# Layer 0 of a two-layer attention kernel: a branch hint on VectorE's loop, and the matmuls of a row in another order

## The chip, the cores and the metric

One core of a Trainium2 chip runs the whole program. The metric is device microseconds from launch to end. The kernel before ran three times: median 5077.78 us (5075.72 to 5081.89). One further execution was profiled: 5074.54 us, with a span of 5072.7 us from its first to its last instruction.

## The reference

The input is an image `x` of 128 channels by 256 by 256. Layer 0 is the stage that changes:

```
n      = layer_norm_over_all(group_norm(x)) * ln_w + ln_b      # 128 x 256 x 256
q, k, v = wq @ n, wk @ n, wv @ n      # over channels: 4 heads of 64, at each image row i and position
g      = sigmoid(wg @ n + wg_b)
bias   = wb @ n                       # 4 x 256 x 256
a      = softmax over m of (q[i, j] . k[i, m] / 8 + bias[h, j, m])
o      = g * (a @ v)
x      = x + wrep @ o + wrep_b
```

The bias of the scores is one table of 4 heads x 256 x 256, the same for all rows. Layer 1 is a second attention (8 heads of 32 channels) over the same image with a group norm before it; it is not touched.

## The kernel before, in words

The program has five stages, one after the other: weights are prepared; a first pass over the image gathers statistics and projects the bias parts; the statistics are finished; `layer0` (L456) works through the 256 image rows; then the statistics of its output are finished and `layer1` (L882) follows.

`layer0` handles one image row (256 positions, 128 channels) at a time. Each engine has a program of its own, a list of calls for "row k" in which a call may belong to row k, k+1, k+2 or k+3. So the engines work on up to four rows at once, and the order of the calls in each engine's `row` function, written out by hand, is the order of its queue. Engines are tied by counting semaphores alone. `over_rows` (L53) unrolls eight rows, peels the first and the last eight, and runs the 30 groups between in a loop; each engine has its own loop and its own branch at the end.

For one row the work is this.

- GpSimd (POOL) makes the normalised row in six steps: `normalise` part 0 subtracts the mean, part 1 multiplies with the inverse deviation, 2 and 3 apply `ln_w` and `ln_b`, 4 and 5 split the result into a high and a low float32r half. It also divides the exponentials by their sums (`divide`, L537, one call for each of the four heads).
- TensorE (PE) makes queries, keys, values and gates (`queries`, `keys`, `values`, `gates`, six matmuls of 256 columns each, since a product of split numbers is three products), then `scores` for a pair of heads (12 matmuls, two heads side by side on 64 rows of the array each), `transposes` of the probabilities of one head (4), `attend` for a pair of heads (two heads side by side on 64 columns each) and `project_out` (6).
- ScalarE (ACT) rounds queries and keys to their high halves (`queries_high`, `keys_high`), copies values, takes the gates' tanh (`gates_out`), the exponentials (`exponents`, two units a head), the high half of the gated result (`output_high`) and two of the four transposed heads (`transposed_out`, heads 0 and 2).
- VectorE (DVE) adds the bias to the scores and takes their maximum (`biased`, two units a head), makes the low halves (`queries_low`, `keys_low`, `output_low`), the reciprocals (`inverse`), the other two transposed heads (`transposed_out`, 1 and 3), the gated product (`gated`), the residual sum (`residual`) and the statistics of the result (`measure`).
- SyncE issues the loads of `x`, `ln_w` and `ln_b` (two rows a transfer, buffers for eight rows) and the stores of the result.

The eight PSUM banks are shared out by hand: bank 0 holds queries and then values (`b_qv`), bank 1 keys and then gates (`b_kg`), banks 2 and 3 the scores of one head each of a pair (`b_s`), banks 4 and 5 the transposes (`b_t`), bank 6 the attend products (`b_av`), bank 7 the output (`b_out`). The second pair's scores wait until the first pair's banks are evacuated, and `probs_t`, the evacuated transposes, has one buffer a head.

PE's order for a row is: attend pair 1 of k; transposes 1 of k+1; scores pair 0, gates of k+2; queries of k+3; attend pair 0 of k+1; scores pair 1 of k+2; transposes 3 and 2 of k+1; keys of k+3; output of k; values of k+3; transposes 0 of k+2.

Of the kernel before, what the change touches and what calls it, by code (L numbers as in the profile page):

```python
# [20 lines left out]
P = 128  # L21
C0 = 128
W = 256
# [21 lines left out]
def loop_ends_peeled(engine, count, body):  # L45

    body(0, True, False)
    with engine.Fori(1, count - 1) as t:
        body(t, False, False)
    body(count - 1, False, True)  # L50

def over_rows(engine, total, unroll, row, ahead=3, behind=1):  # L53

    def body(t, first, last):
        for k in range(-ahead if first else 0, unroll + behind if last else unroll):
            row(t, k, lambda d, k=k: (not first or k + d >= 0) and (not last or k + d < unroll))
    loop_ends_peeled(engine, total // unroll, body)  # L60
# [395 lines left out]
def layer0(nc, m, x, ln_w, ln_b, x1, stats):  # L456

    UNROLL, TILE = 8, 2  # L460
    BUFS = UNROLL // TILE
    AHEAD = 4
    PAIRS = NH0 // 2
    with ExitStack() as ctx:
# [12 lines left out]
        probs_t = sb("probs_t", [P, NH0, KC, W])  # L477
# [8 lines left out]
        b_qv, b_kg = m.psum[0], m.psum[1]  # L486
        b_s, b_t, b_av, b_out = m.psum[2:4], m.psum[4:6], m.psum[6], m.psum[7]
# [9 lines left out]
        av_mm = sems("av_mm", PAIRS)  # L497
# [4 lines left out]
        def rows(engine, row):  # L502
            over_rows(engine, W, UNROLL, row, ahead=AHEAD, behind=1)

# [31 lines left out]
        def _(pool):  # L536
# [59 lines left out]
        def _(pe):  # L596
            def queries(t, k):
# [3 lines left out]
                wait(pe, v_ready, r)  # L601
                for j in range(HC):
                    last = matmul_split(nc, b_qv[:, j * W:(j + 1) * W], [w[:, 0, j] for w in m.wqk], [x_[:, k % 4] for x_ in xn])
# [11 lines left out]
            def values(t, k):  # L615
                r = UNROLL * t + k
                pe.wait_ge(q_ready, r + 1)
                for c in range(KC):
                    last = matmul_split(nc, b_qv[:, c * W:(c + 1) * W], [x_[:, k % 4, c * P:(c + 1) * P] for x_ in xn], [w[:] for w in m.wv_t])
# [9 lines left out]
            def scores(t, k, pair):  # L629
# [9 lines left out]
                for c in range(KC):  # L639
                    for a, b in ((0, 0), (0, 1), (1, 0)):  # L640
                        for j in range(2):
                            channels = slice(j * D0, (j + 1) * D0)
                            last = nc.tensor.matmul(b_s[j][:, c * W:(c + 1) * W], q[a][channels, k % 2, pair, c * P:(c + 1) * P],  # L643
                                                    kk_[b][channels, k % 2, pair], start=a + b == 0, stop=a == 1)
                last.then_inc(s_mm[pair], 1)

            def transposes(t, k, h):
                r = UNROLL * t + k
                pe.wait_ge(p_ready[h], r + 1)
                if h >= 2:  # L650
                    pe.wait_ge(t_ready[h - 2], r + 1)
                else:
                    wait(pe, t_ready[h + 2], r)
                for kc in range(KC):
                    for qc in range(KC):
                        last = nc.tensor.transpose(b_t[h % 2][:, kc * W + qc * P:kc * W + (qc + 1) * P], probs[:, h, qc, kc * P:(kc + 1) * P], m.ident[:])  # L656
                last.then_inc(t_mm[h], 1)

            def attend(t, k, pair):
                r = UNROLL * t + k  # L660
                for j in range(2):
# [3 lines left out]
                for kc in range(KC):  # L665
                    for j in range(2):
                        h = 2 * pair + j
                        last = nc.tensor.matmul(b_av[D0 * j:D0 * (j + 1), pair * W:(pair + 1) * W], v[:, k % 2, kc, h * D0:(h + 1) * D0],  # L668
                                                probs_t[:, h, kc], start=kc == 0, stop=kc == KC - 1)
                last.then_inc(av_mm[pair], 1)  # L670

            def project_out(t, k):
                r = UNROLL * t + k
                pe.wait_ge(o_split, r + 1)
                wait(pe, y_ready, r)
                for c in range(HC):
                    last = matmul_split(nc, b_out[:, 0:W], [w[:, c, :] for w in m.wrep_t], [part[:, c] for part in o_parts], start=c == 0, stop=c == HC - 1)
                last.then_inc(out_mm, 1)

            def row(t, k, has):  # L680
                if has(0):
# [716 lines left out]
```

## Time and profile before

| what | value |
|---|---|
| median of three runs | 5077.78 us |
| profiled execution, time | 5074.54 us |
| profiled execution, span | 5072.7 us |
| PE busy, share of the span | 4726.3 us, 93% |
| DVE busy | 4027.1 us, 79% |
| ACT busy | 3552.5 us, 70% |
| POOL busy | 3459.8 us, 68% |
| mean granted TensorE clock | 0.971 |
| landing of layer 0's loads (`x`, `ln_w`, `ln_b`), median | 2.9, 3.4, 3.6 us |

Busy shares are means over stages with different limits. Layer 0 takes roughly the half of the span that ends near 3003 us. In a timeline a line is one instruction, or some merged ones (x8): its start, its duration, engine, source line, operation and tiles; in brackets how long the engine stood idle before it and what ended that. Durations of neighbours overlap, since an engine takes the next instruction before the last one's result is written: what an instruction costs its queue is the distance from its start to the next start.

### The profile page before, as it was taken

What the parts mean: (1) busy time and instruction counts of PE and PEld (TensorE: products, weight loads), DVE (VectorE), ACT (ScalarE), POOL (GpSimd) and SP (SyncE); (2) the same over time, 40 slices, a digit from 0 to 9 for tenths busy, and PEclk for the clock granted to TensorE, in tenths of its full rate; (3) what the DMA queues carried; (4) which work ended last, traced back from release to release, by engine and by line L of the source; (5) the groups of instructions that cost most, each with busy time, mean ns of one, the idle gap of its engine ahead of it and who ended that gap; (6) DMA issues with size and microseconds to landing.
All of it is one profiled execution on the core that took longest, in us unless ns stands there. A gap on an engine that the chain in (4) does not pass through costs nothing. (4 is left out here: it accounts for less than half of the span.)

```text
span 5072.7 us, 150113 instructions
## 1 busy us (share of the span) xinstructions
PE 4726.3 (93%) x44087; PEld 3890.6 (77%) x44087; DVE 4027.1 (79%) x12779; ACT 3552.5 (70%) x11216; POOL 3459.8 (68%) x5926
## 2 busy tenths in 40 slices
PE   4664999999999999999999979999999999999999
PEld 2332878778787787787877857888888888888887
DVE  4445888888888888888888887888888888888887
ACT  2332888888888888888888856666666666666665
POOL 2333888888788888788878845666666666666665
PEclk8776999999999999999999989999999999999999
DMA  8993111111111111111111101111111111111111
GB/s 329 360 359 135 56 54 51 57 50 58 50 58 51 50 58 50 58 50 55 54 50 58 50 26 48 54 50 50 50 50 50 50 53 53 50 50 50 50 50 44
DMA packets 237474, 383.70 MB, mean 76 GB/s; under 512 B 18756, under 2 KB 156616, under 8 KB 224968
## 3 DMA queue, kind: packets, MB, share of 16 engines
q1 hardware_dynamic: 237256, 381.63, 22.5%
q14 instruction: 183, 1.50, 0.1%
q8 instruction: 35, 0.57, 0.0%
HBM read 309.21 MB, written 72.35 MB: 75 GB/s over the span
## 5 line engine op out<-in xcount | busy, mean ns | idle before, releaser
L1300 POOL TENSOR_SCALAR l_probs<-l_probs,l_inv 128x256 f32<-128x256 f32 x2048 | 943.3, 478 | 737.5 <-DVE l_inv L1205 731.9
L543 POOL TENSOR_SCALAR l_probs<-l_probs,l_inv 128x256 f32<-128x256 f32 x2048 | 982.1, 492 | 475.1 <-DVE l_inv L795 475.1
L1124 ACT ACTIVATE l_probs<-bank,l_neg_max 128x256 f32<-128x256 f32 x2048 | 947.4, 481 | 487.2 <-DVE l_neg_max L1199 487.2
L714 ACT ACTIVATE l_probs<-l_probs,l_neg_max 128x256 f32<-128x256 f32 x2048 | 1012.3, 503 | 6.3 <-DVE l_neg_max L787 6.3
L787 DVE CUSTOM_DVE_ANT_0 l_probs<-bank,bias 128x256 f32<-128x256 f32 x2048 | 749.6, 421 | 263.1 <-PE bank L656 187.0
L1199 DVE TENSOR_REDUCE l_neg_max<-bank 128x2 f32<-128x512 f32 x1024 | 646.1, 683 | 93.4 <-PE bank L1033 93.4
L1212 DVE TENSOR_TENSOR l_probs_t<-bank,bias 128x512 f32<-128x512 f32 x1024 | 674.0, 681 | 36.0 <-PE bank L1043 10.4
L656 PE MATMUL bank<-ident,l_probs 128*128 128x128 f32 x4096 | 603.9, 280 | 1.4 <-POOL l_probs L543 1.1
L668 PE MATMUL bank<-l_probs_t,l_v 128*64 128x256 f32 x4096 | 555.1, 392 | 38.9 <-DVE l_probs_t L809 38.3
L656 PEld LDWEIGHTS bank<-ident,l_probs 128*128 128x128 f32 x4096 | 444.7, 141 | 135.5 <-issue 99.0
L1043 PE MATMUL bank<-ident,l_probs 128*128 128x128 f32 x4096 | 531.8, 273 | 3.4 <-DVE l_probs_t L1212 1.7
L1043 PEld LDWEIGHTS bank<-ident,l_probs 128*128 128x128 f32 x4096 | 460.0, 141 | 6.0 <-POOL l_probs L1300 3.6
L1124 ACT ACTIVATION_READ_ACCUMULATOR l_probs<-bank,l_neg_max 128x1 f32 x2048 | 436.1, 213 | 0.0
L714 ACT ACTIVATION_READ_ACCUMULATOR l_probs<-l_probs,l_neg_max 128x1 f32 x2048 | 399.6, 195 | 0.0
L668 PEld LDWEIGHTS bank<-l_probs_t,l_v 128*64 128x64 f32 x4096 | 251.2, 136 | 189.8 <-issue 85.8
L747 ACT ACTIVATE l_gate<-bank,wg_b_half 128x256 f32<-128x256 f32 x512 | 214.1, 469 | 233.7 <-PE bank L81 233.7
L754 ACT ACTIVATE l_probs_t<-bank 128x512 f32<-128x512 f32 x512 | 301.0, 588 | 95.0 <-PE bank L656 95.0
L643 PE MATMUL bank<-l_k_high,l_q_high 64*128 64x256 f32 x2048 | 343.3, 330 | 13.0 <-DVE l_neg_max L787 13.0
L809 DVE COPY l_probs_t<-bank 128x512 f32<-128x512 f32 x512 | 343.3, 670 | 1.1 <-PE bank L656 1.1
L79 PE MATMUL bank<-l_xn_high,wqk_high 128*128 128x256 f32 x1024 | 309.5, 302 | 25.4 <-POOL l_xn_low L570 25.4
L340 POOL TENSOR_TENSOR fp_x<-fp_x,fp_ln_w 128x2048 f32<-128x2048 f32 x32 | 145.5, 4548 | 263.4 <-DVE chunk_stats L327 263.4
L79 PE MATMUL bank<-l_xn_high,w_qk_high 128*128 128x256 f32 x1024 | 310.5, 303 | 3.5 <-POOL l_xn_low L1289 3.5
(193 smaller groups left out, 14046.6 us busy)
## 6 DMA issues: line engine op xcount, KB each, us to landing
fp_x<-in_x_dram SPq DMA_DIRECT2D x32, 1024.0 KB, 6.9
fp_ln_w<-in_L_conv_ln_w_dram SPq DMA_DIRECT2D x32, 1024.0 KB, 8.9
fp_ln_b<-in_L_conv_ln_b_dram SPq DMA_DIRECT2D x32, 1024.0 KB, 10.5
fp_pair<-in_L_conv_pair_repr_dram SPq DMA_DIRECT2D x32, 1024.0 KB, 12.8
l_x<-in_x_dram SPq DMA_DIRECT2D x128, 256.0 KB, 2.9
l_ln_w<-in_L_conv_ln_w_dram SPq DMA_DIRECT2D x128, 256.0 KB, 3.4
l_ln_b<-in_L_conv_ln_b_dram SPq DMA_DIRECT2D x128, 256.0 KB, 3.6
x<-l_y SPq DMA_DIRECT2D x128, 256.0 KB, 2.0
```

Of the source, the lines that this page charges most:

```text
L79: nc.tensor.matmul(out, lh, rh, start=start, stop=False)
L543: last = nc.gpsimd.tensor_scalar(probs[:, h, c], probs[:, h, c], inv[:, h, c:c + 1], 1.0, ALU.mult, ALU.mult)
L643: last = nc.tensor.matmul(b_s[j][:, c * W:(c + 1) * W], q[a][channels, k % 2, pair, c * P:(c + 1) * P], kk_[b][channels, k % 2, pair], sta ...
L656: last = nc.tensor.transpose(b_t[h % 2][:, kc * W + qc * P:kc * W + (qc + 1) * P], probs[:, h, qc, kc * P:(kc + 1) * P], m.ident[:])
L668: last = nc.tensor.matmul(b_av[D0 * j:D0 * (j + 1), pair * W:(pair + 1) * W], v[:, k % 2, kc, h * D0:(h + 1) * D0], probs_t[:, h, kc], sta ...
L714: last = nc.scalar.activation(probs[:, h, c], probs[:, h, c], ACT.Exp, bias=neg_max[:, h, c:c + 1], scale=-1.0, accum_out=total[:, h, c:c ...
L787: last = nc.vector.tensor_tensor_reduce(out=probs[:, h, c], in0=b_s[h % 2][:, c * W:(c + 1) * W], in1=m.bias0[:, c, h], scale=-1.0, scalar ...
L1043: last = nc.tensor.transpose(b_t[TURNS.index(h) % 2][:, kc * W + qc * P:kc * W + (qc + 1) * P], probs[:, h, qc, kc * P:(kc + 1) * P], m.id ...
L1124: last = nc.scalar.activation(probs[:, h, c], b_s[h % 4][:, c * W:(c + 1) * W], ACT.Exp, bias=neg_max[:, h, c:c + 1], accum_out=total[:, h ...
L1199: nc.vector.tensor_reduce(neg_max[:, h], b_s[h % 4][:].rearrange("p (a c) -> p a c", a=KC), AX.X, ALU.max, negate=True).then_inc(max_ready, 1)
L1212: nc.vector.tensor_tensor(probs_t[:, k % 2, h], b_t[TURNS.index(h) % 2][:].rearrange("p (a c) -> p a c", a=KC), m.bias1[:, :, h], ALU.add) ...
L1300: last = nc.gpsimd.tensor_scalar(probs[:, h, c], probs[:, h, c], inv[:, h, c:c + 1], 1.0, ALU.mult, ALU.mult)
```

## The change

- Scores: one call makes all four heads' scores into four banks (2 to 5), with one semaphore `s_mm` in place of one for each pair. It waits for the evacuation of all four heads of the row before.
- Attend: one call makes all four heads' products, with one semaphore `av_mm`.
- Transposes: one bank (6) in place of two. The transposes of a head wait until the head before (in the order 2, 3, 0, 1) is copied out. `probs_t` has two buffers, by the parity of the row.
- Output: the output projection goes into bank 0, which queries and values use as well (`b_qvo`). Queries wait for the residual sum of two rows back, and the output projection for the values' evacuation two rows ahead.
- All five hand-written orders change. POOL runs five rows ahead (`AHEAD = 5`), keys four rows. The number and the sizes of matmuls, activations and vector operations of a row are the same.

```diff
-def loop_ends_peeled(engine, count, body):
+def loop_ends_peeled(engine, count, body, hinted=None):
+
 
     body(0, True, False)
-    with engine.Fori(1, count - 1) as t:
+    with hinted.Fori(1, count - 1, engines=[engine.engine], hint_back_edge=True) if hinted else engine.Fori(1, count - 1) as t:
         body(t, False, False)
     body(count - 1, False, True)
 
 
-def over_rows(engine, total, unroll, row, ahead=3, behind=1):
+def over_rows(engine, total, unroll, row, ahead=3, behind=1, hinted=None):
 
 
 
     def body(t, first, last):
         for k in range(-ahead if first else 0, unroll + behind if last else unroll):
             row(t, k, lambda d, k=k: (not first or k + d >= 0) and (not last or k + d < unroll))
-    loop_ends_peeled(engine, total // unroll, body)
+    loop_ends_peeled(engine, total // unroll, body, hinted)
...
     UNROLL, TILE = 8, 2
     BUFS = UNROLL // TILE
-    AHEAD = 4
+    AHEAD = 5
+    OUT_BEHIND = 2
     PAIRS = NH0 // 2
...
-        probs_t = sb("probs_t", [P, NH0, KC, W])
+        probs_t = sb("probs_t", [P, 2, NH0, KC, W])
...
-        b_qv, b_kg = m.psum[0], m.psum[1]
-        b_s, b_t, b_av, b_out = m.psum[2:4], m.psum[4:6], m.psum[6], m.psum[7]
+        b_qvo, b_kg = m.psum[0], m.psum[1]
+        b_s, b_t, b_av = m.psum[2:6], m.psum[6], m.psum[7]
...
-        s_mm = sems("s_mm", PAIRS)
+        s_mm, av_mm = sem("s_mm"), sem("av_mm")
...
             def row(t, k, has):
-                if has(2):
-                    normalise(t, k + 2, 4)
-                if has(3):
-                    normalise(t, k + 3, 0)
-                if has(2):
-                    normalise(t, k + 2, 5)
-                if has(0):
-                    divide(t, k, 3)
-                if has(3):
-                    normalise(t, k + 3, 1)
-                if has(0):
-                    divide(t, k, 2)
-                if has(3):
-                    normalise(t, k + 3, 2)
-                if has(1):
-                    divide(t, k + 1, 0)
-                if has(3):
-                    normalise(t, k + 3, 3)
-                if has(1):
-                    divide(t, k + 1, 1)
+                if has(5):
+                    normalise(t, k + 5, 0)
+                if has(4):
+                    normalise(t, k + 4, 4)
+                if has(5):
+                    normalise(t, k + 5, 1)
+                if has(4):
+                    normalise(t, k + 4, 5)
+                if has(2):
+                    divide(t, k + 2, 0)
+                    divide(t, k + 2, 1)
+                if has(5):
+                    normalise(t, k + 5, 2)
+                if has(2):
+                    divide(t, k + 2, 2)
+                    divide(t, k + 2, 3)
+                if has(5):
+                    normalise(t, k + 5, 3)
             rows(pool, row)
...
-                wait(pe, v_ready, r)
+                if isinstance(r, int) and r <= OUT_BEHIND:
+                    wait(pe, v_ready, r)
+                else:
+                    pe.wait_ge(y_ready, r - OUT_BEHIND)
...
             def scores(t, k):
-                for h in range(2):
-                    if pair:
-                        pe.wait_ge(s_ready[h], r + 1)
-                    else:
-                        wait(pe, s_ready[2 + h], r)
+                for h in range(NH0):
+                    wait(pe, s_ready[h], r)
...
             def transposes(t, k, h):
-                if h >= 2:
-                    pe.wait_ge(t_ready[h - 2], r + 1)
-                else:
-                    wait(pe, t_ready[h + 2], r)
+                wait(pe, t_ready[(h - 1) % NH0], r + 1 if h else r)
...
-            def attend(t, k, pair):
-                r = UNROLL * t + k
-                for j in range(2):
-                    pe.wait_ge(t_ready[2 * pair + j], r + 1)
+            def attend(t, k):
+                r = UNROLL * t + k
+                for h in range(NH0):
+                    pe.wait_ge(t_ready[h], r + 1)
...
             def project_out(t, k):
-                wait(pe, y_ready, r)
+                if not isinstance(r, int) or r + OUT_BEHIND < W:
+                    pe.wait_ge(v_ready, r + OUT_BEHIND + 1)
+                else:
+                    pe.wait_ge(y_ready, r)
...
             def row(t, k, has):
-                if has(0):
-                    attend(t, k, 1)
-                if has(1):
-                    transposes(t, k + 1, 1)
-                if has(2):
-                    scores(t, k + 2, 0)
-                    gates(t, k + 2)
-                if has(3):
-                    queries(t, k + 3)
-                if has(1):
-                    attend(t, k + 1, 0)
-                if has(2):
-                    scores(t, k + 2, 1)
-                if has(1):
-                    transposes(t, k + 1, 3)
+                if has(1):
                     transposes(t, k + 1, 2)
-                if has(3):
-                    keys(t, k + 3)
                 if has(0):
                     project_out(t, k)
+                if has(1):
+                    transposes(t, k + 1, 3)
+                if has(3):
+                    gates(t, k + 3)
+                    queries(t, k + 3)
+                if has(1):
+                    attend(t, k + 1)
+                if has(2):
+                    transposes(t, k + 2, 0)
+                if has(3):
+                    scores(t, k + 3)
+                if has(2):
+                    transposes(t, k + 2, 1)
                 if has(3):
                     values(t, k + 3)
-                if has(2):
-                    transposes(t, k + 2, 0)
+                if has(4):
+                    keys(t, k + 4)
             rows(pe, row)
...
             def transposed_out(t, k, h):
                 r = UNROLL * t + k
                 act.wait_ge(t_mm[h], r + 1)
-                wait(act, av_mm[h // 2], r)
-                nc.scalar.activation(probs_t[:, h], b_t[h % 2][:].rearrange("p (a c) -> p a c", a=KC), ACT.Copy).then_inc(t_ready[h], 1)
+                wait(act, av_mm, r - 1)
+                nc.scalar.activation(probs_t[:, k % 2, h], b_t[:].rearrange("p (a c) -> p a c", a=KC), ACT.Copy).then_inc(t_ready[h], 1)
 
             def row(t, k, has):
-                if has(0):
-                    output_high(t, k)
-                if has(2):
-                    gates_out(t, k + 2)
-                if has(3):
-                    queries_high(t, k + 3)
+                if has(3):
+                    keys_high(t, k + 3)
+                if has(1):
+                    transposed_out(t, k + 1, 2)
                 if has(2):
                     exponents(t, k + 2, 0)
                     exponents(t, k + 2, 1)
-                if has(1):
-                    transposed_out(t, k + 1, 2)
-                if has(3):
-                    keys_high(t, k + 3)
+                if has(3):
+                    queries_high(t, k + 3)
                 if has(2):
                     exponents(t, k + 2, 2)
                     exponents(t, k + 2, 3)
                     transposed_out(t, k + 2, 0)
                 if has(3):
+                    gates_out(t, k + 3)
+                if has(1):
+                    output_high(t, k + 1)
+                if has(3):
                     values_out(t, k + 3)
             rows(act, row)
...
-                    last = nc.vector.tensor_tensor_reduce(out=probs[:, h, c], in0=b_s[h % 2][:, c * W:(c + 1) * W], in1=m.bias0[:, c, h], scale=-1.0,
+                    last = nc.vector.tensor_tensor_reduce(out=probs[:, h, c], in0=b_s[h][:, c * W:(c + 1) * W], in1=m.bias0[:, c, h], scale=-1.0,
...
             def row(t, k, has):
-                if has(1):
-                    inverse(t, k + 1, 2)
-                if has(0):
-                    gated(t, k)
-                if has(1):
-                    inverse(t, k + 1, 3)
-                    transposed_out(t, k + 1, 1)
                 if has(2):
                     biased(t, k + 2, 1)
-                    biased(t, k + 2, 0)
-                if has(0):
-                    output_low(t, k)
-                if has(3):
-                    queries_low(t, k + 3)
-                if has(2):
-                    inverse(t, k + 2, 0)
-                    biased(t, k + 2, 3)
-                    biased(t, k + 2, 2)
-                    inverse(t, k + 2, 1)
-                if has(1):
-                    transposed_out(t, k + 1, 3)
+                if has(3):
+                    keys_low(t, k + 3)
                 if has(0):
                     residual(t, k)
-                if has(3):
-                    keys_low(t, k + 3)
+                if has(1):
+                    transposed_out(t, k + 1, 3)
+                if has(2):
+                    inverse(t, k + 2, 0)
+                    biased(t, k + 2, 2)
+                    biased(t, k + 2, 3)
+                if has(3):
+                    queries_low(t, k + 3)
+                if has(2):
+                    inverse(t, k + 2, 1)
                 if has(0):
                     measure(t, k)
-            rows(dve, row)
+                if has(1):
+                    gated(t, k + 1)
+                if has(2):
+                    inverse(t, k + 2, 3)
+                    inverse(t, k + 2, 2)
+                if has(3):
+                    biased(t, k + 3, 0)
+                if has(2):
+                    transposed_out(t, k + 2, 1)
+                if has(1):
+                    output_low(t, k + 1)
+            rows(dve, row, hinted=nc)
```

## Rows read from the trace of the kernel before

**Rows 1.** The page, its first line.

```profile
span 5072.7 us, 150113 instructions
```

**Rows 2.** Busy time of each engine (with its records) in a stretch of layer 0.

```profile
1000.00:2500.00 1500.00, 1466.97 (x13080) 1192.40 (x13080) 1244.17 (x4716) 1222.82 (x3651) 1218.97 (x2130) 1.00 0.17 54
```

**Rows 3.** Timeline of PE: the first matmuls of each block of a steady row.

```profile
1005.41 1.08 PE L668 MATMUL bank<-l_probs_t,l_v 128*64 128x256 f32 x8
1006.43 0.66 PE L656 MATMUL bank<-ident,l_probs 128*128 128x128 f32 x4
1007.01 0.39 PE L643 MATMUL bank<-l_k_high,l_q_high 64*128 64x256 f32 x2
...
1007.71 0.28 PE L643 MATMUL bank<-l_k_high,l_q_low 64*128 64x256 f32 x2
1007.91 0.39 PE L79 MATMUL bank<-l_xn_high,wg_t_high 128*128 128x256 f32 x1
...
1008.73 0.28 PE L79 MATMUL bank<-l_xn_high,wqk_high 128*128 128x256 f32 x1
...
1009.53 1.08 PE L668 MATMUL bank<-l_probs_t,l_v 128*64 128x256 f32 x8
1010.54 0.39 PE L643 MATMUL bank<-l_k_high,l_q_high 64*128 64x256 f32 x2
...
1011.45 1.09 PE L656 MATMUL bank<-ident,l_probs 128*128 128x128 f32 x8
1012.30 0.36 PE L79 MATMUL bank<-l_xn_high,wqk_high 128*128 128x256 f32 x1
...
1013.09 0.28 PE L79 MATMUL bank<-l_o_high,wrep_t_high 128*128 128x256 f32 x1
...
1014.49 0.60 PE L656 MATMUL bank<-ident,l_probs 128*128 128x128 f32 x4
1015.02 1.08 PE L668 MATMUL bank<-l_probs_t,l_v 128*64 128x256 f32 x8
```

**Rows 4.** Timeline of DVE: first instructions of an iteration, and of a later one.

```profile
1047.71 0.17 DVE L795 RECIPROCAL l_inv<-l_total 128x2 f32<-128x2 f32 x1 [2.92 <-issue]
...
1048.53 0.67 DVE L809 COPY l_probs_t<-bank 128x512 f32<-128x512 f32 x1
...
1283.89 0.17 DVE L795 RECIPROCAL l_inv<-l_total 128x2 f32<-128x2 f32 x1 [2.94 <-issue]
```

**Rows 5.** Timeline of PE behind the end of an iteration.

```profile
1049.30 1.08 PE L668 MATMUL bank<-l_probs_t,l_v 128*64 128x256 f32 x8 [1.27 <-DVE l_probs_t L809]
```

**Rows 6.** Waits of DVE, 580 to 3000 us: total, times, longest.

```profile
DVE l_inv L795 <- issue: 85.0, 29, 3.2
```

**Rows 7.** Timeline of DVE in two steady rows.

```profile
1008.17 0.42 DVE L787 CUSTOM_DVE_ANT_0 l_probs<-bank,bias 128x256 f32<-128x256 f32 x1 [0.27 <-PE bank L643]
...
1013.70 0.67 DVE L809 COPY l_probs_t<-bank 128x512 f32<-128x512 f32 x1
1014.29 0.48 DVE L833 SCALAR_TENSOR_TENSOR l_y<-bank,wrep_b,l_x 128x256 f32<-128x256 f32 x1
1014.68 0.68 DVE L803 TENSOR_TENSOR l_k_low<-bank,l_k_high 128x512 fp32r<-128x512 f32 x1
```

**Rows 8.** Timeline of ACT: its copy of a transposed head.

```profile
1012.58 0.60 ACT L754 ACTIVATE l_probs_t<-bank 128x512 f32<-128x512 f32 x1 [0.37 <-PE bank L656]
```

**Rows 9.** `output_low` (L822): min/median/max ns of all 256; one beside POOL's timeline.

```profile
L822 DVE TENSOR_TENSOR l_o_low<-l_o,l_o_high x256: 685/1009/1018, 500.7 to 3002.7; 128x512 fp32r<-128x512 f32 x128
...
1107.47 0.69 DVE L822 TENSOR_TENSOR l_o_low<-l_o,l_o_high 128x512 fp32r<-128x512 f32 x1
...
1107.47 1.03 POOL L543 TENSOR_SCALAR l_probs<-l_probs,l_inv 128x256 f32<-128x256 f32 x1
1108.47 0.74 POOL L561 TENSOR_TENSOR l_xf<-l_xf,l_ln_w 128x256 f32<-128x256 f32 x1
1109.52 0.93 POOL L543 TENSOR_SCALAR l_probs<-l_probs,l_inv 128x256 f32<-128x256 f32 x2 [0.31 <-DVE l_inv L795]
```

More of the change, by code:

```diff
@@ L500, in layer0, with rows @@
         block = ctx.enter_context(nc.Block())
-        def rows(engine, row):
-            over_rows(engine, W, UNROLL, row, ahead=AHEAD, behind=1)
+        def rows(engine, row, hinted=None):
+            over_rows(engine, W, UNROLL, row, ahead=AHEAD, behind=1, hinted=hinted)
         @block.sync
@@ L600, in queries @@
                 pe.wait_ge(xn_ready, r + 1)
-                wait(pe, v_ready, r)
+                if isinstance(r, int) and r <= OUT_BEHIND:
+                    wait(pe, v_ready, r)
+                else:
+                    pe.wait_ge(y_ready, r - OUT_BEHIND)
                 for j in range(HC):
-                    last = matmul_split(nc, b_qv[:, j * W:(j + 1) * W], [w[:, 0, j] for w in m.wqk], [x_[:, k % 4] for x_ in xn])
+                    last = matmul_split(nc, b_qvo[:, j * W:(j + 1) * W], [w[:, 0, j] for w in m.wqk], [x_[:, k % 4] for x_ in xn])
                 last.then_inc(q_mm, 1)
@@ L618, in values @@
                 for c in range(KC):
-                    last = matmul_split(nc, b_qv[:, c * W:(c + 1) * W], [x_[:, k % 4, c * P:(c + 1) * P] for x_ in xn], [w[:] for w in m.wv_t])
+                    last = matmul_split(nc, b_qvo[:, c * W:(c + 1) * W], [x_[:, k % 4, c * P:(c + 1) * P] for x_ in xn], [w[:] for w in m.wv_t])
                 last.then_inc(v_mm, 1)
@@ L627, in gates, with scores @@
                 last.then_inc(g_mm, 1)
-            def scores(t, k, pair):
+            def scores(t, k):
                 r = UNROLL * t + k
@@ L633, in scores @@
                 pe.wait_ge(k_ready, r + 1)
-                for h in range(2):
-                    if pair:
-                        pe.wait_ge(s_ready[h], r + 1)
-                    else:
-                        wait(pe, s_ready[2 + h], r)
-                for c in range(KC):
-                    for a, b in ((0, 0), (0, 1), (1, 0)):
-                        for j in range(2):
[L642 to L645, printed above, removed]
+                for h in range(NH0):
+                    wait(pe, s_ready[h], r)
+                for pair in range(PAIRS):
+                    for c in range(KC):
+                        for a, b in ((0, 0), (0, 1), (1, 0)):
+                            for j in range(2):
+                                channels = slice(j * D0, (j + 1) * D0)
+                                last = nc.tensor.matmul(b_s[2 * pair + j][:, c * W:(c + 1) * W], q[a][channels, k % 2, pair, c * P:(c + 1) * P],
+                                                        kk_[b][channels, k % 2, pair], start=a + b == 0, stop=a == 1)
+                last.then_inc(s_mm, 1)
             def transposes(t, k, h):
@@ L649, in transposes @@
                 pe.wait_ge(p_ready[h], r + 1)
-                if h >= 2:
-                    pe.wait_ge(t_ready[h - 2], r + 1)
-                else:
-                    wait(pe, t_ready[h + 2], r)
+                wait(pe, t_ready[(h - 1) % NH0], r + 1 if h else r)
                 for kc in range(KC):
                     for qc in range(KC):
-                        last = nc.tensor.transpose(b_t[h % 2][:, kc * W + qc * P:kc * W + (qc + 1) * P], probs[:, h, qc, kc * P:(kc + 1) * P], m.ident[:])
+                        last = nc.tensor.transpose(b_t[:, kc * W + qc * P:kc * W + (qc + 1) * P], probs[:, h, qc, kc * P:(kc + 1) * P], m.ident[:])
                 last.then_inc(t_mm[h], 1)
-            def attend(t, k, pair):
+            def attend(t, k):
                 r = UNROLL * t + k
-                for j in range(2):
-                    pe.wait_ge(t_ready[2 * pair + j], r + 1)
+                for h in range(NH0):
+                    pe.wait_ge(t_ready[h], r + 1)
                 pe.wait_ge(v_ready, r + 1)
                 wait(pe, o_ready, r)
[L665 to L670, printed above, removed]
+                for pair in range(PAIRS):
+                    for kc in range(KC):
+                        for j in range(2):
+                            h = 2 * pair + j
+                            last = nc.tensor.matmul(b_av[D0 * j:D0 * (j + 1), pair * W:(pair + 1) * W], v[:, k % 2, kc, h * D0:(h + 1) * D0],
+                                                    probs_t[:, k % 2, h, kc], start=kc == 0, stop=kc == KC - 1)
+                last.then_inc(av_mm, 1)
             def project_out(t, k):
@@ L720, in queries_high @@
                 act.wait_ge(q_mm, r + 1)
-                wait(act, s_mm[1], r - 1)
-                nc.scalar.activation(q[0][:, k % 2], b_qv[:].rearrange("p (h c) -> p h c", h=HC), ACT.Copy).then_inc(q_high, 1)
+                wait(act, s_mm, r - 1)
+                nc.scalar.activation(q[0][:, k % 2], b_qvo[:].rearrange("p (h c) -> p h c", h=HC), ACT.Copy).then_inc(q_high, 1)
             def keys_high(t, k):
@@ L726, in keys_high @@
                 act.wait_ge(k_mm, r + 1)
-                wait(act, s_mm[1], r - 1)
+                wait(act, s_mm, r - 1)
                 nc.scalar.activation(kk_[0][:, k % 2], b_kg[:].rearrange("p (h c) -> p h c", h=HC), ACT.Copy).then_inc(k_high, 1)
@@ L738, in values_out @@
                 act.wait_ge(v_mm, r + 1)
-                wait(act, av_mm[1], r - 1)
-                nc.scalar.activation(v[:, k % 2], b_qv[:].rearrange("p (h c) -> p h c", h=2), ACT.Copy).then_inc(v_ready, 1)
+                wait(act, av_mm, r - 1)
+                nc.scalar.activation(v[:, k % 2], b_qvo[:].rearrange("p (h c) -> p h c", h=2), ACT.Copy).then_inc(v_ready, 1)
             def gates_out(t, k):
```

22 lines of the change are left out of this document (11 added, 11 removed).

## The prediction

> **What bounds the kernel now.** I read the busy time by stretch first, then the timelines of one loop iteration on PE, DVE and ACT, then DVE's waits. In the middle of layer 0, which ends near 3003 us [rows 9], TensorE (PE) is busy 97.8% of the time (1466.97 of 1500 us) at the full granted clock, while VectorE (DVE), ScalarE (ACT) and GpSimd (POOL) each stand at 81 to 83% [rows 2]. So a row costs what PE needs for it, and the others matter where PE waits for them.
>
> A steady row on PE is 9.61 us: from the attend of a second pair at 1005.41 to the next at 1015.02, with no idle between [rows 3]. Eight rows are 76.88 us. An iteration of the loop takes more: DVE's first instruction of one starts at 1047.71 and that of the third after it at 1283.89, which is 78.73 us each [rows 4]. The missing 1.85 us is at the end of the loop body. There DVE stands still for 2.92 us with no releaser ("issue") ahead of the first reciprocal of the next iteration. Its copy of turned probabilities is then late, and PE waits 1.27 us for it [rows 4, 5]. DVE pays this 29 times, 85.0 us in all [rows 6]: the back edges of a loop of 30 iterations. PE has its own copy of the loop and shows no stop at its end.
>
> **The change on PE.** The matmuls stay the same; their order changes, and what one costs depends on its neighbour. From [rows 3], start to start: attend of a pair 1.02 and 1.01; transposes of one head 0.58 after an attend and 0.53 before one, and 0.85 for two heads together, so 0.43 a head among full tiles; scores of a pair 0.90 and 0.91; gates 0.82 after scores; queries 0.80 before attend; keys 0.79 after transposes; output and values 1.40, so 0.70 each behind another projection. Sum: 1.02 + 0.58 + 0.90 + 0.82 + 0.80 + 1.01 + 0.91 + 0.85 + 0.79 + 1.40 + 0.53 = 9.61.
>
> New order, by those rows: transposes of head 2, 0.43; output after transposes 0.79; transposes 3, 0.43; gates 0.79; queries before attend 0.80; all attend products 1.87; transposes 0, 0.58; all scores 1.61; transposes 1, 0.43; values 0.79; keys 0.70. For the attend products I take one pair's 1.01 and add its four inner steps of about 0.215, the longer first and last steps being paid once; for the scores 0.91 and six unbroken steps of 0.117 (0.70 us lie between the first and the last of six, 1007.01 and 1007.71, the first step being the longer one by 0.1). Sum 9.22. The 0.39 us come from fewer changes between tiles of 64 rows, 64 columns and full size, less two more starts behind transposes. Four score banks also free the second pair from the evacuation of the first, but in a steady row nothing waits for that now.
>
> The Trainium skill, "TensorEngine Tiling (Array Packing)", says that changing the tiling mode drains TensorE. The trace agrees: these are the places where a step is some 0.1 us longer.
>
> **What then is late.** At 9.22 us a row I place the other queues against PE's, each instruction at its predecessor's start plus its interval. Three chains come near.
>
> First, the one bank for transposes. ACT must have copied head 2's out before head 3's are made, and only the output projection lies between: 1.22 us from start to start. The copy starts 1.13 us after a block of eight transposes (1011.45 to 1012.58 [rows 3, 8]), so 0.70 after one of four; it takes 0.60, and its release 0.1 at most: 1.38. PE loses 0.16, and a row is at least 9.38 us. The other three handoffs have over 1.4 us of other work between.
>
> Second, DVE. Its queue is now: biased 1, keys_low, residual, copy 3, inverse 0, biased 2 and 3, queries_low, inverse 1, measure, gated, two inverses, biased 0 of the next row, copy 1, output_low, and round to biased 1. Gates on PE wait for keys_low, which stands behind four instructions that start only when the scores of the row before are there. Once round: gates' start to scores' start 0.79 + 0.80 + 1.87 + 0.58 = 4.04; scores' start to biased 0, 1.61 - 0.21 + 0.46 = 1.86 (last score matmul to DVE, 1007.71 to 1008.17 [rows 3, 7]); biased 0, 0.69 (four units from 1008.17, two heads, in 1.38: output_low starts at once behind); copy 0.59 (1013.70 to 1014.29); output_low x; biased 1, 0.69; keys_low 0.68 [rows 7]; DVE's end to PE's start 0.10 (copy at 1048.53 plus 0.67, attend at 1049.30 [rows 4, 5]). Together 8.65 + x. Queries_low ends about 3.0 us after gates' start, 1.0 before scores want it, and copy 3 some 0.5 before attend does, so neither decides. ACT and POOL are busy 8.0 us of a row of 9.84 on average [rows 2] and keep over 1 us of gap.
>
> What is x? output_low reads two operands from SBUF. It takes 0.69 at least (0.60 to the next start) and mostly 1.009 (0.92) [rows 9]. In one fast case it starts together with a division on POOL, which then takes 1.03 alone, where two take 0.93 a little later: one of the two stands still. So x lies between 0.60 and 0.92. In the new order output_low falls beside normalise 3 and 0, back to back on POOL, so I take 0.85, nearer the row that is seen most. A row is then 9.50.
>
> The Trainium skill, "SBUF — State Buffer", section "SBUF: two separate sides", calls the port pair that DVE and GpSimd share an exclusive lock, held for the whole instruction. The trace's pair agrees; by that rule output_low could wait for a whole GpSimd instruction, which is the slow rival below.
>
> Third, the output projection of a row waits for its output_low, with only transposes 2 ahead; by the same placement it is released 0.25 us late, inside the 0.28 that PE would lose to keys_low anyway. Output and queries share a bank now; residual ends 0.5 us before queries want it, and nothing is lost there.
>
> **The hint**, if it works, takes DVE's gap away: 29 x 1.85 = 53.7 us off. Something may stay, since the branch now lies in the chain that binds (between output_low and biased 1). No row shows it: below, nothing; above, 0.45, a small part of today's gap; I take 0.2, 5.8 us in all. **The ends:** POOL works five rows ahead instead of four and keys four instead of three, so one more short row fills the pipeline: between 0 and one row, 9; I take 3. **Loads** for a row go out seven rows ahead as now and are first read five rows ahead instead of three. Two rows, 19 us, remain for a landing of a few us, so they cost nothing; without that cover a late landing would stop POOL, then keys.
>
> **Sum.** Rows: 256 x 0.11 = 28.2 off. Hint: 53.7 - 5.8 = 47.9 off. Ends +3. Net -73.1 against the profiled execution's 5074.5 (span 5072.7 [rows 1] and 1.8 around it), 5001.4. The median of the runs lies 3.3 above that execution, so 5005.
>
> **Rivals.**
> *DVE's chain does not bind.* With output_low alone, x = 0.60 gives 9.25, and the transposes' handoff sets 9.38: 256 x 0.23 = 58.9, plus 53.7, less 3: 4968. Against it: 1.009 is the median of 256. Were that handoff hidden too, 9.22 would give 4927.
>
> *The gap stays at the back edge.* DVE has 30 records a row there, ACT 23, POOL 14 [rows 2], and only DVE's gap shows; the hint may bring the branch's target and leave the part behind it missing. Then 2.94 lies in the binding chain: 29 x (2.94 - 1.85) = 31.6 more, less 28.2, plus 3: 5084. For it: no slack on DVE in the new order. Against it: the gap is at the branch and nowhere else now.
> The Trainium skill, "Runtime: NRT & Kernel Launch", section "Instruction fetch mechanics", says that a taken branch to a target outside the two blocks held pays a fetch, and names no remedy.
>
> *Slower: DVE waits for whole POOL instructions.* If output_low meets the start of a POOL instruction of 0.74 us each row [rows 9], x = 1.34 and a row is 9.99: 256 x 0.38 = 97.3, less 47.9, plus 3: 5130. It decides from a row of 9.82, x = 1.17, where the hint is used up. Against it: no output_low took over 1.018.
>
> *A row of 9.6 to 9.75:* one or two handoffs 0.1 longer than placed, 26 us each: 5030 to 5069.
>
> **Chances.** Forecast 0.50 (its own range 4980 to 5030), chain not binding 0.15 and all hidden 0.04, row of 9.6 to 9.75 0.12, gap stays 0.12, whole POOL instructions 0.07. The range 4960 to 5068 leaves out 0.04 below and at most 0.16 above. A measurement of this kernel can tell some 0.2%, 10 us: faster, below 5068, 0.81; same 0.09 (most of the gap's case); slower 0.10.
>
> **What the profile after would show.** Right: no DVE gap with "issue" once in eight rows; a wait of PE of about 0.3 us a row ahead of gates or output, released by DVE; output_low near 1.0 us; layer 0 some 70 us shorter and layer 1 the same. Wrong: PE idle ahead of transposes 3 on ACT alone (the first chain binds); a wait of scores on queries_low; a DVE gap near 2.9 us every 76; or a gap of ACT's or POOL's own at the back edge, which DVE's would hide today.

## The result, and the profile after

The changed kernel takes 5214.96 us (median of four runs, 5198.22 to 5219.51) against 5079.55 for the kernel before: a ratio of 1.0261, with a 95% interval of 1.0236 to 1.0286. It is 2.6% slower, where 1.5% faster was forecast, and the time lies far outside the range. The profiled execution took 5219.51 us, with a span of 5217.4. One execution of a run below, the one without the hint, took 5542.28 us at a mean granted TensorE clock of 0.82 in place of 0.95, and is left out of its median.

The busy time (with records) of PE, its weight loads, DVE, ACT and POOL in the same stretch of layer 0 as in [rows 2]; the column before the last two is the granted clock:

```profile
1000.00:2500.00 1500.00, 1394.41 (x12402) 1168.31 (x12400) 1260.29 (x4470) 1152.63 (x3458) 1135.34 (x2020) 0.97 0.16 50
```

PE does 12402 matmul records there in place of 13080, and stands at 93% in place of 97.8%. Who keeps it waiting is told by the first line of PE's waits, 500 to 3200 us (total, times, longest):

```profile
PE bank L80 <- DVE l_o_low L821: 182.3, 113, 2.4
```

Before, no such wait stood in layer 0's steady rows. `output_low` is L821 now. Its line, which answers to the first of [rows 9] (min/median/max ns):

```profile
L821 DVE TENSOR_TENSOR l_o_low<-l_o,l_o_high x256: 682/748/3187, 506.0 to 3144.9; 128x512 fp32r<-128x512 f32 x128
```

The median has fallen from 1.009 to 0.748 us and the maximum has risen from 1.018 to 3.187. So the median says nothing here; the longest ones do. Below, an output_low that takes longer because of POOL is called locked out. Two rows of the same execution, from the timelines of DVE and, below the dots, of POOL:

```profile
1065.66 0.73 DVE L821 TENSOR_TENSOR l_o_low<-l_o,l_o_high 128x512 fp32r<-128x512 f32 x1
...
1065.10 0.74 POOL L565 TENSOR_TENSOR l_xf<-l_xf,l_ln_b 128x256 f32<-128x256 f32 x1
1065.80 1.19 POOL L557 TENSOR_TENSOR l_xf<-l_x,mean 128x256 f32<-128x256 f32 x1
```

```profile
1020.83 3.19 DVE L821 TENSOR_TENSOR l_o_low<-l_o,l_o_high 128x512 fp32r<-128x512 f32 x1
...
1020.29 0.75 POOL L565 TENSOR_TENSOR l_xf<-l_xf,l_ln_b 128x256 f32<-128x256 f32 x1
1020.99 0.74 POOL L557 TENSOR_TENSOR l_xf<-l_x,mean 128x256 f32<-128x256 f32 x1
1021.68 0.41 POOL L570 TENSOR_SCALAR l_xn_high<-l_xf 128x256 fp32r<-128x256 f32 x1
1022.05 0.73 POOL L561 TENSOR_TENSOR l_xf<-l_xf,rstd 128x256 f32<-128x256 f32 x1
1022.74 0.73 POOL L572 TENSOR_TENSOR l_xn_low<-l_xf,l_xn_high 128x256 fp32r<-128x256 f32 x1
```

In both, output_low starts 0.54 to 0.56 us behind the start of POOL's normalise 3 (L565). In the first it goes ahead of POOL's next instruction, normalise 0, which then takes 1.19 us in place of 0.74. In the second POOL's next four instructions (normalise 0, 4, 1 and 5) all go first, each at its usual length, and output_low takes its own 0.69 us only when this unbroken run ends. PE, which has nothing ahead of the output projection but head 2's transposes, waits for it:

```profile
1024.07 0.38 PE L80 MATMUL bank<-l_o_high,wrep_t_high 128*128 128x256 f32 x1 [2.31 <-DVE l_o_low L821]
```

From the starts of the 250 successive output_lows between 560 and 3145 us, by their length:

| output_low takes | rows | to the next output_low |
|---|---|---|
| 0.7 to 0.8 us | 140 | 9.36 to 9.46 us, mostly 9.37 (less in the layer's last rows) |
| 1.1 to 1.3 | 16 | 9.73 to 9.88 |
| 1.4 | 26 | 10.03 |
| 3.2 | 68 | 12.68 on average |

The 26 of 1.4 us were passed by one POOL instruction, and the 16 came at the start of normalise 0 and waited for it alone. The rows of the 68 are longer than by their 2.5 us of delay because PE's granted clock fell in some of them: in 25 it stayed at 1.00 and the row took 11.8 us, in 43 it was 0.87 over the row, which took 13.0 to 13.3. Busy time and granted clock behind one wait of each kind:

```profile
1024.00:1027.50 3.50, 3.43 (x28) 3.02 (x30) 3.50 (x16) 1.52 (x5) 0.93 (x2) 1.00 0.22 75
1037.00:1040.50 3.50, 3.50 (x19) 2.98 (x19) 2.51 (x12) 1.00 (x5) 0.93 (x2) 0.51 0.00 0
```

The second stretch is at the lower level, 1.2 GHz, after PE had stood still for 2.31 us; the first is at 2.4 GHz after a wait just as long.

Against rows of 9.37 us the sum is 68 x 3.31 + 26 x 0.66 + 16 x 0.42 = 249 us. Taken from 5215 that leaves 4966; the first rival stood at 4968. The experiments had to show whether this sum is real.

### The profile page after: what moved, and what is told of

Same layout as the page of the kernel before. It is cut to its first block and busy times, and to the rows that moved or that the text cites. A ratio compares the mean times of both kernels' runs of the same rounds, so it can differ in the third digit from the quotient of the medians.

```text
span 5217.4 us, 149629 instructions
## 1 busy us (share of the span) xinstructions
PE 4734.8 (91%) x44087; PEld 3959.4 (76%) x44087; DVE 4169.1 (80%) x12779; ACT 3544.6 (68%) x11216; POOL 3422.6 (66%) x5926
## 5 line engine op out<-in xcount | busy, mean ns | idle before, releaser
L1301 POOL TENSOR_SCALAR l_probs<-l_probs,l_inv 128x256 f32<-128x256 f32 x2048 | 943.7, 478 | 737.4 <-DVE l_inv L1206 731.9
L545 POOL TENSOR_SCALAR l_probs<-l_probs,l_inv 128x256 f32<-128x256 f32 x2048 | 947.8, 478 | 652.5 <-DVE l_inv L794 652.3
L654 PE MATMUL bank<-ident,l_probs 128*128 128x128 f32 x4096 | 659.8, 285 | 5.1 <-ACT l_probs_t L753 1.6
L1044 PE MATMUL bank<-ident,l_probs 128*128 128x128 f32 x4096 | 532.4, 273 | 2.9 <-DVE l_probs_t L1213 1.5
L667 PE MATMUL bank<-l_probs_t,l_v 128*64 128x256 f32 x4096 | 503.5, 388 | 2.2 <-DVE l_probs_t L808 2.2
L667 PEld LDWEIGHTS bank<-l_probs_t,l_v 128*64 128x64 f32 x4096 | 274.0, 138 | 151.7 <-issue 10.4
L821 DVE TENSOR_TENSOR l_o_low<-l_o,l_o_high 128x512 fp32r<-128x512 f32 x256 | 383.3, 1497 | 0.7 <-ACT l_o_high L733 0.7
L80 PE MATMUL bank<-l_o_high,wrep_t_high 128*128 128x256 f32 x512 | 174.9, 342 | 182.3 <-DVE l_o_low L821 182.3
L739 ACT ACTIVATE l_v<-bank 128x512 f32<-128x512 f32 x256 | 153.7, 600 | 270.3 <-PE bank L82 270.3
L644 PE MATMUL bank<-l_k_high,l_q_high 64*128 64x256 f32 x2048 | 315.5, 305 | 2.3 <-DVE l_q_low L798 2.3
L80 PE MATMUL bank<-l_xn_high,wqk_high 128*128 128x256 f32 x1024 | 292.7, 286 | 26.2 <-POOL l_xn_low L572 26.2
## 6 DMA issues: line engine op xcount, KB each, us to landing
fp_pair<-in_L_conv_pair_repr_dram SPq DMA_DIRECT2D x32, 1024.0 KB, 11.8
```

Of the source, the lines that this page charges most:

```text
L80: nc.tensor.matmul(out, lh, rh, start=start, stop=False)
L545: last = nc.gpsimd.tensor_scalar(probs[:, h, c], probs[:, h, c], inv[:, h, c:c + 1], 1.0, ALU.mult, ALU.mult)
L654: last = nc.tensor.transpose(b_t[:, kc * W + qc * P:kc * W + (qc + 1) * P], probs[:, h, qc, kc * P:(kc + 1) * P], m.ident[:])
L821: nc.vector.tensor_tensor(o_parts[1][:], o[:], o_parts[0][:].bitcast(F32), ALU.subtract).then_inc(o_split, 1)
L1044: last = nc.tensor.transpose(b_t[TURNS.index(h) % 2][:, kc * W + qc * P:kc * W + (qc + 1) * P], probs[:, h, qc, kc * P:(kc + 1) * P], m.id ...
L1301: last = nc.gpsimd.tensor_scalar(probs[:, h, c], probs[:, h, c], inv[:, h, c:c + 1], 1.0, ALU.mult, ALU.mult)
```

## The experiments

All ratios are to the kernel before, run on the same chip in the same rounds.

**The hint taken out of the changed kernel.**

```diff
-            rows(dve, row, hinted=nc)
+            rows(dve, row)
```

> The changed kernel with the branch hint taken out. Theory A (output_low is locked out by POOL's unbroken run in about 68 of 256 rows, and that is the whole loss): the 2.9 us gap comes back at 29 back edges in DVE's binding queue, so about 29 x 2.9 = 84 us on top of 5215, near 5300; but POOL runs dry in such a gap, so some lockouts of the rows behind it may go and it may be as low as 5240. Theory B (the hint itself disturbs the loop): as fast as or faster than the changed kernel, 5215 or below.

5366.50 us (median of three, 5366.17 to 5378.63), ratio 1.0575 (1.0554 to 1.0596). The hint is no culprit: without it the kernel loses another 152 us. That is more than 84, and the forecast that some lockouts would go was wrong. There are more of them: of 250 output_lows here 90 take 3.0 to 3.2 us and 96 take 1.4, and against rows of 9.37 the sum is 397 us, 148 more than in the changed kernel. DVE's gap at the back edge is in this sum, but only 21.5 us of it, in 19 places. Why the gap brings more lockouts was not tested; that it shifts DVE against POOL is a guess.

**The hint alone, on the kernel before.** The two helper functions change as in the diff of the change, and then

```diff
-            rows(dve, row)
+            rows(dve, row, hinted=nc)
```

> The kernel before with nothing but the branch hint on the vector engine's loop of layer 0. Both theories of the loss in the row order leave this alone: 29 x 1.85 = 54 us off, 5024, and no gap with issue in DVE's waits. If the hint is what costs (theory B): no faster than before, 5078 or more.

5021.21 us, ratio 0.9886 (0.987 to 0.9903): 60 us off (5080.85 less 5021.21) where 54 were forecast. PE is never idle in the stretch, and every row takes 9.6 us. The hint by itself is worth 1.1%, and DVE's wait with "issue" is gone:

```profile
1000.00:2500.00 1500.00, 1500.00 (x13429) 1218.98 (x13429) 1262.91 (x4843) 1255.66 (x3747) 1264.75 (x2187) 1.00 0.17 55
```

**POOL yields.** POOL's first step for the row five ahead (normalise 0) waits until output_low is done.

```diff
                     wait(pool, xn_ready, r - 1)
+                    if isinstance(r, int):
+                        wait(pool, o_split, r - 4)
+                    else:
+                        pool.wait_ge(o_split, r - 4)
```

> The changed kernel; POOL's first step for a row five ahead also waits until output_low of the present row is done, so that POOL's run has a break just where output_low stands. Same work. Theory A: no output_low over 1.2 us, rows at 9.4 us, the whole at 4965 to 4990, faster than both kernels. Theory C (the long output_low only shows a queue that is bound by the single transpose bank or by gates behind keys_low): PE's waits move to another instruction and the time stays above 5150.

4975.26 us, ratio 0.9793 (0.9777 to 0.981). The wait added to POOL makes the kernel 240 us faster than the changed one, and 106 faster than the one before (5080.85 in these rounds). No output_low takes over 0.93 us. POOL waits 168.2 us in all for it and has the room: it still stands still for reciprocals (284.0 us):

```profile
L825 DVE TENSOR_TENSOR l_o_low<-l_o,l_o_high x256: 680/728/930, 510.3 to 2904.2; 128x512 fp32r<-128x512 f32 x128
```

```profile
POOL l_probs L545 <- DVE l_inv L798: 284.0, 256, 4.0
POOL l_xf L561 <- DVE l_o_low L825: 168.2, 245, 0.7
```

**One operand from PSUM.** The orders stay as they are; output_low's first operand lies in PSUM. It is the product without the gate, so this kernel leaves the gate out of the low half and serves only to measure time. Attend waits for output_low in place of `gated`, since the bank is now read until then.

```diff
-                wait(pe, o_ready, r)      # attend
+                wait(pe, o_split, r)
...
-                nc.vector.tensor_tensor(o_parts[1][:], o[:], o_parts[0]...
+                nc.vector.tensor_tensor(o_parts[1][:], b_av[:]..., o_parts[0]...
```

> The changed kernel, with output_low reading the ungated product from its PSUM bank in place of the gated one from SBUF, so that it has one SBUF input; it leaves the gate out of the low half. Size and queue are the same. Theory A in the form that only an instruction with two SBUF inputs is locked out: output_low is 0.7 us in every row, rows at 9.4 us, 4965 to 4985. If POOL holds back any DVE instruction at that place, or the queue is the cause (theory C): the long ones stay and the time stays near 5215.

4971.78 us, ratio 0.9786 (0.977 to 0.9803). All 256 take 0.68 to 0.69 us. In 252 of them output_low starts during normalise 3, at the median 0.55 us into it as in the changed kernel, and the same unbroken run of POOL follows:

```profile
L821 DVE TENSOR_TENSOR l_o_low<-bank,l_o_high x256: 680/681/692, 509.1 to 2898.1; 128x512 fp32r<-128x512 f32 x128
```

So what holds output_low back is its second SBUF operand, and with one alone the kernel is 243 us faster. Theory C is out by both runs. The Trainium skill, "SBUF — State Buffer", section "SBUF: two separate sides", names just this class, a DVE instruction "with two SBUF inputs" against a GpSimd instruction that reads SBUF, as one that takes the shared pair; the run agrees.

**A shorter run of POOL.** Normalise 3 and 0 stay together; the three steps after them go behind the division of head 0.

```diff
                 if has(5):
                     normalise(t, k + 5, 0)
+                if has(2):
+                    divide(t, k + 2, 0)
                 if has(4):
                     normalise(t, k + 4, 4)
...
                 if has(2):
-                    divide(t, k + 2, 0)
                     divide(t, k + 2, 1)
```

> The changed kernel, with POOL's order altered so that only two instructions (normalise 3 and normalise 0) stand between the place where output_low arrives and POOL's next wait (the division of head 0); the other three follow behind that division. Same work. If a locked-out output_low gets its turn only when POOL runs dry, the longest one shrinks from 3.2 to about 1.4 to 2.3 us, and the time falls from 5215 to between 5000 and 5060. If the 3.2 us are a fixed penalty, or do not depend on POOL's queue, they stay and so does the time.

5267.72 us, ratio 1.037 (1.0352 to 1.0387). The length came out as forecast and the time did not. The longest output_low shrank with the run, from 3.2 us to 2.0 in nearly every row and 2.3 at most; a fixed penalty is out. But now output_low is locked out in 245 of 250 rows instead of 110, and a row takes 10.57 us. One row, DVE then POOL:

```profile
1003.92 1.98 DVE L822 TENSOR_TENSOR l_o_low<-l_o,l_o_high 128x512 fp32r<-128x512 f32 x1
...
1003.92 0.75 POOL L565 TENSOR_TENSOR l_xf<-l_xf,l_ln_b 128x256 f32<-128x256 f32 x1
1004.62 0.73 POOL L557 TENSOR_TENSOR l_xf<-l_x,mean 128x256 f32<-128x256 f32 x1
1008.42 0.93 POOL L545 TENSOR_SCALAR l_probs<-l_probs,l_inv 128x256 f32<-128x256 f32 x2 [3.07 <-DVE l_inv L795]
```

1003.92 + 1.98 - 0.69 = 1005.21, which is 0.14 us before the recorded end of the last instruction of the run (1005.35); in the long row above it is 1020.83 + 3.19 - 0.69 = 1023.33 against 1023.47. A long-delayed output_low gets its turn when POOL's run ends, whether that has two instructions or four behind it. And a lockout that comes every row costs more than a longer one in every fourth: 256 x 1.2 us against 68 x 3.3. I had priced the length and left out that in the new order output_low also arrives elsewhere, at the very start of normalise 3.

**The hint in the new order, with nothing locked out.** The kernel in which POOL yields, and

```diff
-            rows(dve, row, hinted=nc)
+            rows(dve, row)
```

> The kernel in which POOL yields to output_low (4975 us), without the branch hint. It measures what the hint is worth in the new order when nothing is locked out. By the prediction's term (the whole gap of 2.94 us lies in a queue without slack) 29 x 2.9 = 85 us, 5060. The few rows of 11.0 us in the run without hint speak for 29 x 1.6 = 46 us instead, 5021, since the sequencer reaches the branch while the long instructions ahead of it still run.

5018.29 us, ratio 0.9878 (0.9861 to 0.9894): 43 us above the kernel with the hint, so the second number held. DVE's gap is 1.65 us there and not 2.9:

```profile
DVE l_probs L790 <- issue: 47.8, 29, 1.8
```

The gap is counted from the end of the instruction ahead. Before, that was the last of four short statistics (0.59 us together); here it is an output_low of 0.75 us behind a copy of 0.69. That part of the stop is hidden under these is a guess which no run tests by itself.

**Head 2's transposes in a free score bank**, on top of the kernel in which POOL yields.

```diff
-                wait(pe, t_ready[(h - 1) % NH0], r + 1 if h else r)
+                if h == 2:
+                    pe.wait_ge(s_ready[0], min(r + 2, W) if isinstance(r, int) else r + 2)
+                elif h == 3:
+                    pe.wait_ge(t_ready[1], r + 1)
+                else:
+                    wait(pe, t_ready[(h - 1) % NH0], r + 1 if h else r)
+                bank = b_s[0] if h == 2 else b_t
```

The scores also wait for ACT's copy of head 2.

> The kernel in which POOL yields (4975 us), with head 2's transposes in the first score bank, which is free from biased 0 until the next scores; so transposes 3 no longer wait for ACT's copy of head 2. If the handoff of the one transpose bank sets the 9.37 us of a row, as the prediction's first chain has it, a row falls to between 9.25 and 9.33 us (PE's own 9.22, the vector queue 8.65 + 0.65) and the time to 4945 to 4965. If the vector queue or PE's own work sets the 9.37, it stays at 4975.

4958.18 us, ratio 0.9758 (0.9742 to 0.9775), with rows of 9.33 in place of 9.38 us. Before this edit (the run in which POOL yields) the trace shows the handoff itself, head 2's transposes at 1008.17 and head 3's at 1009.60, 1.43 us apart where PE's own work was placed at 1.22 and the handoff at 1.38:

```profile
1008.17 0.60 PE L658 MATMUL bank<-ident,l_probs 128*128 128x128 f32 x4
...
1009.60 0.63 PE L658 MATMUL bank<-ident,l_probs 128*128 128x128 f32 x4
```

**POOL yields one instruction earlier.** On top of the last kernel; the wait for output_low stands before normalise 3 in place of normalise 0.

```diff
                 elif part == 3:
+                    wait(pool, o_split, r - 3)
```

> The kernel with head 2's transposes in a score bank (4958 us, rows of 9.33), with POOL yielding one instruction earlier: normalise 3 waits for output_low, so output_low also meets no running POOL instruction and takes 0.69 in place of 0.75. If the vector queue sets the row there, a row falls by the 0.06 to the 9.25 to 9.28 of its sum and the time to 4940 to 4950; if PE's own work sets it, the row stays at 9.33 and the time at 4958.

4940.07 us, ratio 0.973 (0.9714 to 0.9746), the fastest of all: 2.7% under the kernel before, 5.3% under the changed one. Output_low takes 0.68 us, and the next one starts at 1015.60, a row of 9.27 us later. Head 3's transposes now follow head 2's after 1.22 us.

```profile
1006.33 0.68 DVE L829 TENSOR_TENSOR l_o_low<-l_o,l_o_high 128x512 fp32r<-128x512 f32 x1
```

## Why the prediction was wrong

The step that failed is the question "What is x?", the price of output_low in DVE's queue. I wrote that x lies between 0.60 and 0.92, from the shortest and the median output_low of [rows 9], and took 0.85. In the changed kernel x was 1.44 on average over 250 rows: 0.67 in 140 of them, below what I took, and 3.11 in 68, far above the bound. The slow rival had the right mechanism, place and direction, with 7% for it, but its price was capped at one POOL instruction, x = 1.34. I had seen that normalise 3 and 0 stand back to back, and used it only to choose inside the range. The maximum of 1.018 that I held against the rival belonged to the old neighbourhood of output_low and said nothing of the new one.

The old neighbourhood did not lack long runs. Most rows before had one POOL instruction behind the division that output_low met, but in 29 of 246 steady rows five followed without a stop, and output_low still waited for a single division, 0.91 to 0.92 us in all. One of these rows of the kernel before, DVE then POOL:

```profile
656.94 0.92 DVE L822 TENSOR_TENSOR l_o_low<-l_o,l_o_high 128x512 fp32r<-128x512 f32 x1
...
656.84 1.36 POOL L543 TENSOR_SCALAR l_probs<-l_probs,l_inv 128x256 f32<-128x256 f32 x2
```

POOL goes on without a stop to 660.51 there. So a long run is needed for a long lockout, but does not bring one by itself. Before, output_low came in beside a division; in the new order it comes in beside normalise 3 or 0. Whether the kind of POOL instruction that it meets decides, or the moment, no run separates. What is shown is that it takes the second SBUF operand, and that a stop of POOL at this place ends it.

Point by point:

- PE's new order. Forecast 9.22 us of PE's own work. The fastest kernel's rows are 9.27, so at least 0.34 of the 0.39 us is there.
- First chain, one transpose bank: a row of at least 9.38. Rows without a lockout take 9.37 in the changed kernel, and removing the handoff gave 9.33. Right in the row. The handoff itself was placed at 1.38, though its own terms (0.70, 0.60 and at most 0.1) give up to 1.40, and measured 1.43.
- Second chain, 8.65 + x. With x as the traces have it, from output_low's start to the next start, it gives 9.32 for 0.67 (head 2 in a score bank, measured 9.33), 9.25 for 0.60 (the fastest kernel, 9.27), 10.56 for 1.91 (the shorter run of POOL, 10.57) and 11.76 for 3.11 (the changed kernel's lockouts at full clock, 11.77). Right to 0.02 us.
- Third chain, the output projection behind output_low: I had it hidden inside the loss to keys_low. It is the place where PE waits, since it stands 1.2 us ahead of gates in PE's queue. Both hang on output_low, and the second chain's sum gives the row all the same.
- The hint. 53.7 us forecast on the old order, 60 measured; 47.9 in the new order, 43 measured where nothing is locked out. Its removal there puts 1.65 us in the queue and not 2.94, so that rival was priced too high.
- The ends. Forecast 3 us; the first output_low starts at 506.0 in place of 500.7 us, 5.3 later.
- Layer 1: unchanged, as forecast (PE 98% busy from 3150 to 5200 us; from the last output_low to the end 2072.5 us, 2070.0 before).
- The chances. Gap stays and whole POOL instructions both lie above 5068 and have 0.19 together, not "at most 0.16". And a row has 31 records on DVE and 24 on ACT, not 30 and 23. Neither moves the forecast.

Against 5005: with x = 0.67, 9.32, the first chain's 9.38 sets the row, which is the first rival's 4968. Two runs without lockouts found 4975 and 4972; the lockouts add 240 to 243.

## What to carry to other kernels

When an order puts a VectorE instruction with two SBUF operands in the queue that binds, look at what GpSimd runs beside it. Take the whole unbroken run of GpSimd's instructions as the upper bound of its delay, not one of them and not the old trace's maximum. Where GpSimd has slack, a wait of GpSimd for that instruction is the cure: 240 us here, and a little more with the wait one instruction earlier. An operand from PSUM does it too, where the kernel has it there. A median over all instances hides such a loss; look at minimum, median and maximum side by side.

## What the runs showed of the hardware

- A VectorE instruction with two SBUF operands can wait through POOL's whole run: 2.5 us with four more instructions behind the one it met, 1.3 us with one more. By its usual 0.69 us it then starts 0.14 us before the run's recorded end. It can also get in after one instruction (1.4 us) or at once. With one operand from PSUM it took 0.68 to 0.69 us in all 256 rows at the same place.
- The Trainium skill, "SBUF — State Buffer", section "SBUF: two separate sides", has the pair go to the one that starts first, "for the whole instruction". It does not say who gets it next; one instruction's wait would be 0.74 us at most here. The 2.5 us measured decide.
- Who wins is a matter of hundredths of a microsecond, or of something that the records do not show. Starting 0.54 to 0.57 us behind the start of normalise 3, output_low was sometimes next, sometimes one instruction late (1.4) and sometimes last (3.2). What settles it stays open: the recorded starts of the three kinds overlap.
- After a PE pause of 2.31 us the granted clock fell to the lower level in 43 rows and not in 25, which made a row of 11.8 us one of 13.2.
